# One of four mask products of a cross attention to GpSimd, and the last operation of its norm from GpSimd to ScalarE

## What is computed

```python
    q = _split_heads(query @ Wq.T + bq)      # 16 heads of 8 features
    k = _split_heads(key @ Wk.T + bk)
    v = _split_heads(value @ Wv.T + bv)
    scores = jnp.einsum('bhqd,bhkd->bhqk', q, k) * SCALE
    scores = jnp.where(mask == 0, NEG_INF, scores)
    attn = jax.nn.silu(scores)
    out = jnp.einsum('bhqk,bhkd->bhqd', attn, v)
    return out.transpose(0, 2, 1, 3).reshape(B, Sq, HIDDEN) @ Wo.T
```

## Time and profile before

| | |
|---|---|
| median of 3 runs | 1946.37 us (1945.16 to 1950.12) |
| the profiled execution | 1942.95 us |
| its span, first to last instruction | 1941.2 us |
| the stage of the change | about 1518 to 1661 us of the span |
| DMA | 25.74 MB, a mean of 13 GB/s |
| granted TensorE clock | 0.995 of full speed |

### The profile page before, as it was taken

The page is one execution under the profiler, slowest core; times in us unless marked ns, Lnnn a source line. Parts: engine busy times, 40 slices in busy tenths (PEclk is TensorE's granted clock), DMA queues, the critical chain, the costliest instruction groups (busy, mean ns, idle before and its releaser), DMA issues.

```text
span 1941.2 us, 48644 instructions
## 1 busy us (share of the span) xinstructions
PE 1863.6 (96%) x17206; PEld 1493.1 (77%) x17206; DVE 1418.5 (73%) x3593; ACT 1213.4 (63%) x4022; POOL 560.9 (29%) x894
## 2 busy tenths in 40 slices
PE   7999999999999999999989999999999899899998
PEld 6888888888888888887867777767777566677775
DVE  6678788887888888777757666679888899545443
ACT  2677677676776777878645444458888777233333
POOL 2222223223223231112122211124555477211100
PEclk9999999999999999999999999999999999999999
DMA  7100000000000000000000000000000400000000
GB/s 225 43 2 2 2 2 2 2 2 2 1 2 2 2 2 2 2 2 2 2 1 1 1 1 1 1 2 13 2 3 2 132 18 3 1 1 11 12 6 17
DMA packets 30230, 25.74 MB, mean 13 GB/s; under 512 B 5276, under 2 KB 26788, under 8 KB 29992
## 3 DMA queue, kind: packets, MB, share of 16 engines
q1 hardware_dynamic: 29992, 22.62, 4.0%
HBM read 20.52 MB, written 2.10 MB: 12 GB/s over the span
## 4 chain that ended last, share of the span: by engine, by line
issue 48%; PE 24%; POOL 15%; POOLq 9%; SPq 2%; DVE 1%; DMA 0%; DVEq 0%; ACT 0%; ACTq 0%
PE bank L1318 6%; PE bank L1310 5%; POOL X L2134 3%; POOL work L1119 3%; PE bank L2247 2%; PE bank L2234 2%; PE bank L2236 2%; SPq L2508 2%; POOLq L1122 2%; POOL wbig L1888 2%; POOLq L1096 1%; POOL H L1123 1%; POOL X L1898 1%; POOL work L1097 1%; PE bank L1273 1%
## 5 line engine op out<-in xcount | busy, mean ns | idle before, releaser
L782 ACT ACTIVATE work<-bank,work 128x128 f32<-128x128 f32 x1024 | 363.1, 402 | 195.8 <-DVE work L880 195.8
L551 PE MATMUL bank<-work,wbig 128*128 128x128 f32 x2048 | 260.1, 275 | 3.0 <-ACT work L845 3.0
L551 PEld LDWEIGHTS bank<-work,wbig 128*128 128x128 f32 x2048 | 243.8, 192 | 3.5 <-ACT work L845 3.2
L782 ACT ACTIVATION_READ_ACCUMULATOR work<-bank,work 128x1 f32 x1024 | 246.3, 241 | 0.0
L887 DVE TENSOR_TENSOR work<-work 128x512 f32<-128x512 f32 x256 | 178.9, 699 | 20.1 <-issue 1.3
L797 ACT ACTIVATE work<-bank 128x512 f32<-128x512 f32 x256 | 168.6, 658 | 29.5 <-PE bank L564 29.5
L880 DVE TENSOR_REDUCE work<-bank 128x4 f32<-128x512 f32 x256 | 159.1, 685 | 33.6 <-PE bank L590 33.6
L564 PE MATMUL bank<-ident,work 128*128 128x128 f32 x1024 | 158.3, 277 | 17.9 <-DVE work L887 17.7
L564 PEld LDWEIGHTS bank<-ident,work 128*128 128x128 f32 x1024 | 113.9, 141 | 67.1 <-issue 38.9
L1387 ACT ACTIVATE work<-bank,col_b 128x512 f32<-128x512 f32 x128 | 87.4, 688 | 106.9 <-PE bank L1310 106.7
L1117 POOL TENSOR_TENSOR work<-work,lneps 128x1 f32<-128x1 f32 x64 | 15.5, 241 | 479.3 <-DVE work L1059 479.3
(11 more groups left out here) (344 smaller groups left out, 4079.8 us busy)
## 6 DMA issues: line engine op xcount, KB each, us to landing
wbig<-in_moe_w SPq DMA_DIRECT2D x2, 1536.0 KB, 10.0
work<-in_mask_l SPq DMA_DIRECT2D x8, 256.0 KB, 3.0
out<-X SPq DMA_DIRECT2D x8, 256.0 KB, 2.3
H<-in_moe_w SPq DMA_DIRECT2D x3, 512.0 KB, 7.6
wff<-in_moe_w SPq DMA_DIRECT2D x1, 1024.0 KB
X<-in_x SPq DMA_DIRECT2D x1, 512.0 KB, 4.2
wbig<-in_sa_wq SPq DMA_DIRECT2D x1, 512.0 KB, 3.7
wbig<-in_sa_wk SPq DMA_DIRECT2D x1, 512.0 KB, 4.6
```

What stands on the lines that cost most here:

```text
L551: last = nc.tensor.matmul(o[:, j * T:(j + 1) * T], w[:, t * 128:(t + 1) * 128], src, start=True, stop=True)
L782: last = nc.scalar.activation(at_probs[:, g, h, :], bank[g][:, h * T:(h + 1) * T], ACT.Exp, bias=at_nmax[:, g, h:h + 1], accum_out=at_den[ ...
```

## The change

Three things are edited. VectorE multiplies quarters 1, 2 and 3 of a batch with the mask, and GpSimd quarter 0 (`mask_first`), counted by a semaphore of its own, for which `weigh` waits in addition. GpSimd no longer writes the normed batch: it makes `lx_shift` = -mean x rstd (128 x 1), and ScalarE writes scale x input + bias into X (`normal`), at the end of its step, for batch t-2. GpSimd's order becomes mask_first(b), inverse(b-1), with the conversion still ahead of both. Further lines merge semaphores to make room for the new ones (`tables_sb` into `tables`, `shifted` and `chosen` into `choice`); they wait for the same events as before.

```diff
@@ attnx_pe
             def weigh(b):
-                pe.wait_ge(lx.masked, QUADS * (b + 1))
+                pe.wait_ge(lx.masked, 3 * (b + 1))
+                pe.wait_ge(lx.masked_pool, b + 1)
@@ attnx_act
+            def normal(b):
+                act.wait_ge(lx.rstd, b + 1)
+                nc.scalar.activation(X[:, b, :], lx_res[b % 2], ACT.Identity, bias=lx_shift[b % 2][:, 0:1],
+                                     scale=lx_rstd[b % 2][:, 0:1]).then_inc(lx.normed, 1)
...
             def turned(b):
                 act.wait_ge(lx.turned, b + 1)
-                need(act, lx.masked, QUADS * (b - 3))
+                need(act, lx.masked, 3 * (b - 3))
+                need(act, lx.masked_pool, b - 3)
...
                     keys(t + 2)
+                if t >= 2:
+                    normal(t - 2)
+            normal(B - 1)
@@ attnx_dve
-                    for i in range(QUADS):
+                    for i in (1, 2, 3):
                         mask(t, i)
@@ attnx_pool
-            def mask(n):
-                lx_mask(pool, n)
-
-            for b in range(B):
-                if b % NB == 2 and b // NB + 2 < NIT:
-                    mask(b // NB + 2)
+            def mask_first(b):
+                pool.wait_ge(lx.silu, QUADS * b + 1)
+                w = lx_w[b % 2][:, 0, :, :]
+                nc.gpsimd.tensor_tensor(w, w, lx_xcm[b % 4][:, 2, :].unsqueeze(1).to_broadcast([128, QUADS, T]),
+                                        ALU.mult).then_inc(lx.masked_pool, 1)
+
+            def inverse(b):
                 pool.wait_ge(lx.stats, b + 1)
+                need(pool, lx.normed, b - 1)
...
-                nc.gpsimd.tensor_scalar(X[:, b, :], lx_res[b % 2], lx_mv[b % 2][:, 0:1], lx_rstd[b % 2][:, 0:1],
-                                        ALU.subtract, ALU.mult).then_inc(lx.normed, 1)
+                nc.gpsimd.tensor_scalar(lx_shift[b % 2], lx_mv[b % 2][:, 0:1], lx_rstd[b % 2][:, 0:1], -1.0,
+                                        ALU.mult, ALU.mult).then_inc(lx.rstd, 1)
+
+            def mask(n):
+                lx_mask(pool, n)
+
+            for b in range(B):
+                if b % NB == 2 and b // NB + 2 < NIT:
+                    mask(b // NB + 2)
+                mask_first(b)
+                if b >= 1:
+                    inverse(b - 1)
+            inverse(B - 1)
```

More of the change, by code:

```diff
@@ L222, in build @@
             tables_ready = sem("l1_tables_ready")
-            tables_sb = sem("l1_tables_sb")
             tables_w = sem("l1_tables_w")
@@ L260, in build @@
             masked = sem("lx_masked")
+            masked_pool = sem("lx_masked_pool")
+            rstd = sem("lx_rstd")
             pv = sem("lx_pv")
@@ L272, in build @@
             logits = sem("g1_logits")
-            shifted = sem("g1_shifted")
+            choice = sem("g1_choice")
             exps = sem("g1_exps")
-            chosen = sem("g1_chosen")
             counts = sem("g1_counts")
@@ L1660, in tokens @@
                 if t == -3:
-                    pe.wait_ge(l1.tables_sb, 1)
+                    pe.wait_ge(l1.tables, 2)
                     pe.wait_ge(l1.tables_w, 1)
@@ L1804, in l1_tables_second @@
                 last = nc.vector.memset(l1_ones[:, k, DH1 * k:DH1 * (k + 1)], 1.0)
-            last.then_inc(l1.tables_sb, 1)
+            last.then_inc(l1.tables, 1)
             dve.drain()
@@ L1928, in build @@
         lx_rstd = [r.take(1) for _ in range(2)]
+        lx_shift = [r.take(1) for _ in range(2)]
         lx_slot = r.take(QUADS)
@@ L2122, in attnx_pool @@
         def attnx_pool(pool):
+            def mask_first(b):
[4 more added lines that the diff above has]
+            def inverse(b):
+                pool.wait_ge(lx.stats, b + 1)
+                need(pool, lx.normed, b - 1)
+                nc.gpsimd.tensor_tensor(lx_var, lx_mv[b % 2][:, 1:2], lneps[:, 0:1], ALU.add)
+                pool.drain()
+                nc.gpsimd.tensor_tensor(lx_rstd[b % 2], lx_var, half[:, 0:1], ALU.pow)
+                pool.drain()
+                nc.gpsimd.tensor_scalar(lx_shift[b % 2], lx_mv[b % 2][:, 0:1], lx_rstd[b % 2][:, 0:1], -1.0,
+                                        ALU.mult, ALU.mult).then_inc(lx.rstd, 1)
             def mask(n):
@@ L2271, in tail1_pe @@
             idle_passes(95, bank[7])
-            pe.wait_ge(g1.chosen, 1)
+            pe.wait_ge(g1.choice, 2)
             nc.tensor.matmul(bank[5][:, 0:B * E1], upper[:, :], g1_chosen[:, :], start=True, stop=True)\
@@ L2333, in tail1_act @@
                 routed_copy(act, b)
-            act.wait_ge(g1.shifted, 1)
+            act.wait_ge(g1.choice, 1)
             nc.scalar.activation(probs1, g1_shifted, ACT.Exp).then_inc(g1.exps, 1)
@@ L2363, in route @@
                 dve.drain()
-                nc.vector.tensor_tensor(g1_shifted, raw, spread(g1_max), ALU.subtract).then_inc(g1.shifted, 1)
+                nc.vector.tensor_tensor(g1_shifted, raw, spread(g1_max), ALU.subtract).then_inc(g1.choice, 1)
                 dve.wait_ge(g1.exps, 1)
@@ L2374, in route @@
                 dve.drain()
-                nc.vector.tensor_copy(g1_chosen, g1_eq.rearrange("p b e -> p (b e)")).then_inc(g1.chosen, 1)
+                nc.vector.tensor_copy(g1_chosen, g1_eq.rearrange("p b e -> p (b e)")).then_inc(g1.choice, 1)
                 dve.wait_ge(g1.counts, 1)
```

## The result

| | before | after |
|---|---|---|
| median | 1946.72 us (1945.16 to 1950.12, 11 runs) | 1952.02 us (1949.41 to 1954.07, 11 runs) |
| profiled execution, span | 1942.95, 1941.2 us | 1952.02, 1950.3 us |
| granted TensorE clock | 0.995 | 0.992 |

The ratio is 1.0031 (95% interval 1.0023 to 1.0038), the two medians are 5.3 us apart (1.0027): the changed kernel is slower, by a little. The page's busy times answer to the earlier trace rows.

A forecast was written before the change was run, and what follows sets the result against it. VectorE was taken to set the pace at 4.19 us a step, with a ring of waits at 4.14 next; -1.6 + 0.2 + 3.3 + 5.1 = +7.0 us on 1946.4 gave 1953.4 us, range 1945.5 to 1960.

The forecast's parts named there:

- the port: VectorE's two-SBUF-input products and GpSimd's SBUF-reading instructions keep each other out; half of 30 steps x 0.22 = +3.3 us.
- the conversions: Six batches where GpSimd's mask conversion delays mask_first and so TensorE's weighting; 6 x 0.85 = +5.1 us.
- the stage's end: Last batch: TensorE gets back its 0.41 us wait for products; GpSimd's and ScalarE's new norm operations add +0.2 us.
- the ring: Closed loop of scores, silus, heads' copy, output product and next scores, untouched by the change; holds steps at 4.14 us.
- the term said 1.2: Gain in steady steps from relieving VectorE, 4.19 to 4.14 us: 0.05 us in some 24 steps, 1.2 us.
- the bound from the first block: From the first block's routing: a GpSimd product keeps a VectorE product of two SBUF inputs out for up to 0.89 us.
- the two phases: GpSimd's third operation either meets VectorE's products, leaving mask_first free, or precedes mask_first, which then holds VectorE for 0.89 us.
- the signs named for the new profile: Single VectorE products of 1.3 to 1.6 us, six weighting waits over 1 us, steps 4.1 to 4.4, one near 5 in four.
- The rule weighed against it: SBUF-reading instructions exclude each other throughout: conversion holds VectorE 2.0 us, product 1.04, sum some +12; the forecast followed the trace.
- Rival (b): VectorE kept out for a conversion's whole 2.01 us, then the product, within one set of products: +12, 1958.5 us; chance 0.15.
- ScalarE's operation: The norm's last operation moved to ScalarE: about 0.31 us, falling where ScalarE waits for scores, so costing nothing in the steps.

The follow-up runs named there:

- e6: Changed kernel without quarter 0's mask product, VectorE doing three and nobody the first, so part of the computation is left out: 1946.13 us, ratio 0.9995.
- e9: Changed kernel without quarter 0's mask product, and with ScalarE's heads' copy between third and fourth silu: 1936.96 us, ratio 0.9952 to the kernel before.
- e7: Changed kernel with GpSimd filling quarter 0 twice with zeros instead of multiplying, so it reads no SBUF there: 1946.96 us, ratio 0.9998.
- e5: Changed kernel with the last batch's four products on VectorE and the conversion behind mask_first and inverse: 1949.64 us, ratio 1.0012 to the kernel before.
- e2: Changed kernel with the mask conversion moved behind mask_first(b) and inverse(b-1): 1948.78 us, ratio 1.0014 to the kernel before.
- e1: Changed kernel with all four mask products of the last batch on VectorE: 1949.65 us, ratio 1.0019 to the kernel before.
- e3: Norm's part of the change alone, all four mask products on VectorE and no mask_first: 1946.0 us, ratio 1.0001 to the kernel before.

## Why the prediction was right, and where only its total was

The forecast of a median 7.0 us higher met 5.3; the stage alone is 6.3 longer in the traces. The sign and the port were foreseen. That the total came so near is luck: two terms were wrong by about as much, the conversions too high and the stage's end too low.

- **The bound and the ring: right.** 4.14 us holds in e6 to 0.01. Removing the product was worth 129.14 - 128.09 = 1.05 us in the steps, the term said 1.2. e9 shows that ScalarE's order is in the ring.
- **The port: right in kind, phase and size.** The kind is shown by e7, which does all but read. One blocking in mid-stage costs 0.82 us, the bound from the first block was 0.89. Besides batch 2's, twelve steps are over 4.14: seven beside a product, by 0.25 to 0.31 us, 2.0 in all, and five beside a conversion, by 0.07 or 0.08, 0.4 in all. The term was 3.3 for fifteen steps of 0.22. In e5, where the conversions have the late place, the same difference to e7 is 130.95 - 128.10 = 2.85 us.
- **The conversion: wrong in size.** The term was 6 x 0.85 = 5.1 us. In the changed kernel batch 2 costs 1.45 us, and the other five conversions cost less than the products in whose place they meet VectorE; putting all six behind the product wins 1.0 (e2, and e5 against e1). Three inputs were off. GpSimd's operation on one column takes 0.27 us when nobody is in its way; 0.66 had been worked out from two other forms, of 128 columns with two one-column operands and of 256 with one. The conversion does not hold the port for 1.35 us: begun 0.15 us ahead of the products at 1602.67, it made them 2.21 - 1.90 = 0.31 us longer, so it kept VectorE out for its first 0.46 us. And the prediction took one value between the two phases for all six, while five fell into the one in which the small operation ahead runs free, and the first into the other. So of the signs named for the new profile those of the port came (single products of about 1.5 us, steady steps of 4.1 to 4.4), and those of the conversion (six waits of the weighting over 1 us, one step near 5 in four) came once, at batch 2.
- **The rule weighed against it.** The Trainium skill, "SBUF — State Buffer", section "Who interferes with whom", has a GpSimd instruction that only writes leave VectorE alone; e7 agrees, with 1.90 us beside two fills. Its exclusion for the whole instruction fits the product nearly (begun 0.12 us ahead, it kept VectorE out up to 0.95 of its 1.09 us) and not the conversion (up to 0.46 of 1.94). Rival (b), built on it, is refuted; the 0.41 of 2.38 in e3 says the same.
- **The end: wrong.** The prediction had the last batch win 0.4 us and lose 0.2. It lost 3.5. Its step "in the last batch TensorE waits 0.41 us and gets that back" looked at VectorE alone; GpSimd's product was not followed into the last batch, where TensorE has no scores and projections of another batch to do while it waits. e1 gives 3.1 us back. Of the loss 1.1 us is the wait (5.50 - 4.39), 1.94 - 1.09 = 0.85 the weighting and 3.99 - 2.35 = 1.64 the fillers at the lower clock, 3.6 in all.
- **ScalarE's operation** takes 0.49 us, not 0.31. It is hidden, as the prediction said: e6 has it in each of its steps of 4.14.

In the steps, then, the changed kernel wins 1.04 us (from before to e7) and loses 1.45 at batch 2 and 2.38 in the twelve steps, which is the 131.93 - 129.14 = 2.79 measured.

Of what is left in e5, 142.57 - 140.44 = 2.1 us of the stage, 2.85 - 1.04 = 1.8 is the port less the gain in the steps, and 0.3 lies at the end.

Three things stay open. Why the end is 1.7 us shorter in e2 (13.17 us, not 14.85): its last weighting waits 1.29 us, not 1.52, and the lower clock lasts 3.4 us, not 6.8, but no run shows which of the two brings the other. The clock at the end isn't the last product's doing alone: e6 and e7 have 3.4 us of the lower level there with waits of 0.29 us before the last weighting, e1 with 0.50 and e3 with 0.40 have none between it and the barrier. So that the wait brought the clock down in the changed kernel is argued, not shown; shown is that both go with GpSimd's last product. And 2.55 us of the spans' difference lie ahead of everything edited; each kernel was traced once, so how much of a median such stretches are is not known.

## What to carry to other kernels

Before giving an engine a share of a loop's work, find the closed ring of waits that remains: here it capped the gain at 0.05 us a step, while the cost had no such cap. In these traces VectorE's products with two operands in SBUF hardly overlapped with GpSimd's reading product, so such a move pays only if the two can be kept apart in time, and then the later one must still be early enough. Work that comes once in several steps is to be followed in the phase in which it really falls; here five of six conversions cost next to nothing and one cost 1.45 us. Follow the moved work into the last iteration, where its cover is gone: here 1.1 us of waiting came with 2.5 us of lower clock.

## What the runs showed of the hardware

- What a GpSimd instruction keeps out depends on its kind: a product of 1.09 us, begun 0.12 us ahead, cost VectorE 0.82, a conversion of int32 to float of 1.94 us, begun 0.15 ahead, 0.31, and two fills nothing.
- VectorE's products in a row hardly let GpSimd in: its one-column operation took 0.99 us beside them and 0.27 alone, its product 1.54 and 1.09.
- A wait of 1.5 us before the last weighting was followed by 6.8 us at 1.2 GHz, in which weighting and fillers took 2.5 us more; the wait itself was 1.1 us longer than before.
